# A graph network kernel on one Trainium2 core: paired filter loads and a reordered GRU stage

## The reference

```python
h = relu(_bn(_conv1d(xc, conv1_w, 0), ...))
h = _bn(_conv1d(h, conv2_w, 8), ...)              # 17 taps along the nodes
x_conv = transpose(relu(h + xc), (0, 2, 1))
s = x @ w_se.T + b_se                             # 3 columns
dist = sq[:, :, None] + sq[:, None, :] - 2.0 * einsum('bnd,bmd->bnm', s, s)
A = exp(-dist) * mask
msg = relu(x @ w_msg.T + b_msg)
x_nmp = einsum('bnm,bmd->bnd', A, msg)
x_in = concatenate([x_conv, x_nmp], axis=-1)
gi = x_in @ w_ih.T + b_ih
gh = x @ w_hh.T + b_hh
r, z = sigmoid(gi_r + gh_r), sigmoid(gi_z + gh_z)
nn_ = tanh(gi_n + r * gh_n)
x = _layernorm(x + (1.0 - z) * nn_ + z * x)
```

## Time and profile before

| | |
|---|---|
| median of 3 runs | 2246.25 us |
| profiled execution | 2246.6 us, span 2244.8 us |
| busy PE, PEld | 2039.8 us (91%), 1745.0 us (78%) |
| busy DVE, ACT, POOL | 1470.5 us (66%), 1175.7 us (52%), 676.7 us (30%) |
| product stage, first to last matmul start | 773.9 to 1007.6 us |
| GRU stage, first scores to end | 1021.8 to 2244.8 us |
| mean granted clock of TensorE | 0.974 of 2.4 GHz |

### The profile page before, as it was taken

How to read it: one execution, slowest core, us unless ns; L and a number is a source line. 1 busy time by engine, 2 the same in 40 slices (tenths; PEclk the granted TensorE clock), 3 DMA queues, 4 the chain that set the end, 5 groups by cost and what they waited for, 6 DMA issues and landing times.

```text
span 2244.8 us, 38042 instructions
## 1 busy us (share of the span) xinstructions
PE 2039.8 (91%) x11782; PEld 1745.0 (78%) x11782; DVE 1470.5 (66%) x2709; ACT 1175.7 (52%) x2174; POOL 676.7 (30%) x563
## 2 busy tenths in 40 slices
PE   6888788885988789884999999999999999999997
PEld 5877687774888677774888888888888888888886
DVE  5999797996777666654555655565656565555564
ACT  6888687874555566553344444444444444434342
POOL 5887686873000000000222222222222222222222
PEclk9999999997999999996999999999999999999999
DMA  4655565564222387774112112121212121212110
GB/s 143 220 203 203 191 211 212 213 220 168 80 80 84 88 238 231 230 211 160 45 58 75 66 66 74 58 77 54 78 53 78 53 78 53 78 53 80 67 38 19
DMA packets 208069, 263.07 MB, mean 117 GB/s; under 512 B 12939, under 2 KB 159089, under 8 KB 203761
## 3 DMA queue, kind: packets, MB, share of 16 engines
q1 hardware_dynamic: 207984, 262.14, 35.2%
HBM read 174.01 MB, written 88.08 MB: 117 GB/s over the span
## 4 chain that ended last, share of the span: by engine, by line
PE 52%; issue 1%; ACT 1%; DMA 1%; DVE 0%; SPq 0%; POOL 0%; POOLq 0%; ACTq 0%; DVEq 0%
PE c_ps_g L1386 36%; PE c_ps_s L1413 5%; PE c_ps_m L1386 4%; PE c_ps_s L1386 2%; PE c_ps_s L1457 1%; PE c_ps_y L1436 1%; PE c_ps_y L1473 1%; PE c_ps_m L1473 1%; DMA c_yf<-y_spec 1%; PE c_ps_m L1474 0%; PE c_ps_y L1474 0%; ACT c_wi_h L1147 0%; SPq L1038 0%; SPq L1046 0%; DVE c_t L1255 0%
## 5 line engine op out<-in xcount | busy, mean ns | idle before, releaser
L1209 POOL TENSOR_TENSOR c_cl<-c_xc,c_ch 128x512 fp32r<-128x512 f32 x64 | 82.6, 1291 | 488.2 <-ACT c_ch L1101 470.8
L1285 DVE TENSOR_SCALAR c_work<-c_work 128x512 f32<-128x512 f32 x64 | 27.4, 427 | 219.3 <-ACT c_work L1096 219.3
L833 PE MATMUL m_ps<-m_wh,m_xl 128*128 128x256 f32 (+1 forms) x406 | 136.4, 336 | 35.1 <-issue 16.8
L1386 PE MATMUL c_ps_g<-c_xh,c_wh_l 128*128 128x512 f32 x384 | 155.6, 405 | 4.2 <-POOL c_cl L1209 4.2
L1386 PE MATMUL c_ps_g<-c_ch,c_wi_l 128*128 128x512 f32 x384 | 153.9, 401 | 0.0
L1386 PE MATMUL c_ps_g<-c_xl,c_wh_h 128*128 128x512 f32 x384 | 152.4, 397 | 0.0
L1386 PE MATMUL c_ps_g<-c_ch,c_wi_h 128*128 128x512 f32 x384 | 152.1, 396 | 0.0
L1386 PE MATMUL c_ps_g<-c_nh,c_wi_l 128*128 128x512 f32 x384 | 151.9, 396 | 0.0
L1386 PE MATMUL c_ps_g<-c_xh,c_wh_h 128*128 128x512 f32 x384 | 151.9, 396 | 0.0
L1386 PE MATMUL c_ps_g<-c_cl,c_wi_h 128*128 128x512 f32 x384 | 151.7, 395 | 0.0
L1386 PE MATMUL c_ps_g<-c_nl,c_wi_h 128*128 128x512 f32 x384 | 151.7, 395 | 0.0
(11 more groups left out here) (226 smaller groups left out, 7095.9 us busy)
## 6 DMA issues: line engine op xcount, KB each, us to landing
w_spec<-a_spec SPq DMA_DIRECT2D x32, 1088.0 KB, 11.0
m_w<-w_spec SPq DMA_DIRECT2D x68, 512.0 KB, 3.8
a_xt<-in_x_t SPq DMA_DIRECT2D x64, 256.0 KB
a_xn<-in_x_n SPq DMA_DIRECT2D x64, 256.0 KB, 9.3
x_t<-a_x1t SPq DMA_DIRECT2D x64, 256.0 KB, 9.7
s_x<-x_t SPq DMA_DIRECT2D x64, 256.0 KB, 3.0
y_spec<-m_y SPq DMA_DIRECT2D x64, 256.0 KB, 2.4
c_x<-x_t SPq DMA_DIRECT2D x32, 512.0 KB, 3.9
```

The costliest lines, as they stand in the source:

```text
L833: last = nc.tensor.matmul(out.rearrange("p r (q c) -> p r q c", q=CHUNKS), xx[:, v, c, part], ww[:, v, c].rearrange("p q r c -> p r q c")[ ...
L1209: nc.gpsimd.tensor_tensor(cl[:, v, j], xc[:, j], ch[:, v, j].bitcast(F32), ALU.subtract).then_inc(s_cl, 1)
L1285: nc.vector.tensor_scalar(zz[:, :], tz[:, :], 0.5, 0.5, ALU.mult, ALU.add).then_inc(s_zz, 1)
L1386: last = nc.tensor.matmul(out, stationary, moving, start=(n == 0), stop=(n == len(passes) - 1))
```

## The change

In the product stage the filters of two slots are loaded at once (1 MB, 1 KB pieces in place of 512 B) into one of two buffers of a pair. The high and low parts get three buffers, so that the parts of slot s wait for the products of slot s - 3. In a step, ACT makes `m_xh` and `m_wh` before it copies `m_y`, and DVE makes `m_wl` before it subtracts. SP stores slot i - 5 in step i instead of slot i - 3. The unroll is 12 in place of 4.

In the GRU stage the inverse of one half is made of 256-column products: yh against the high and low parts of the transform side by side, yl against the high part, and the first four frequencies of two graphs in one product with 96 rows. It writes `c_ps_m` in place of `c_ps_s`. DVE adds its two halves in two operations onto x1 with the shift already added (`c_xs`, on ACT, behind the n tanh). DVE makes `c_cl`, and the result from three operations without POOL. The distances get 27 rows of fp32r in place of 9 of fp32, for which ACT makes high parts and DVE stacked rows. A gate takes the message part ahead of the x_conv part, with a wait of its own ahead of each in the first R gate. The first inverse stands behind the Z gate of half 0, the second behind IN of half 1.

```diff
-        w = sb("w", [P, BUFS, KD, CHUNKS, 2, CW])
-        wh = sb("wh", [P, 2, KD, CHUNKS, 2, CW], F32R)
...
+        w = sb("w", [P, BUFS // 2, KD, CHUNKS, 2, 2, CW])
+        wh = sb("wh", [P, SPLIT, KD, CHUNKS, 2, CW], F32R)
...
-                    sp.dma_start(w[:, u].rearrange("p t q r c -> p (t q) (r c)"),
-                                 w_spec.rearrange("n p d c -> p n d c")[:, :, bass.ds(2 * i, 2)].rearrange("p n d c -> p n (d c)")
-                                 ).then_inc(s_w[u], 16)
...
-                    s, b = i - 3, (u - 3) % BUFS
+                if u % 2 == 0 and live(0):
+                    reached(sp, s_wl, i - BUFS + 2)
+                    sp.dma_start(w[:, u % BUFS // 2].rearrange("p t q s r c -> p (t q) (s r c)"),
+                                 w_spec.rearrange("n p d c -> p n d c")[:, :, bass.ds(2 * i, 4)].rearrange("p n d c -> p n (d c)")
...
             def step(i, u, k, live):
+                if live(1):
+                    s, b, v = i - 1, (u - 1) % BUFS, (u - 1) % SPLIT
+                    reached(act, s_m, s - SPLIT + 1)
+                    nc.scalar.activation(xh[:, v], x_spec[:, :, bass.ds(s, 1)].rearrange("p c o r g -> p c (o r) g"), ACT.Copy).then_inc(s_xh, 1)
+                    reached(act, s_w[b // 2], (turns(k, u, 1) + 1) * 16)
+                    nc.scalar.activation(wh[:, v], w[:, b // 2, :, :, b % 2], ACT.Copy).then_inc(s_wh, 1)
...
                     nc.scalar.activation(y[:, b], ps[:, b, 0], ACT.Copy).then_inc(s_yc, 1)
-                if live(1):
-                    s, b, v = i - 1, (u - 1) % BUFS, (u - 1) % 2
-                    reached(act, s_m, s - 1)
-                    nc.scalar.activation(xh[:, v], x_spec[:, :, bass.ds(s, 1)].rearrange("p c o r g -> p c (o r) g"), ACT.Copy).then_inc(s_xh, 1)
-                    at_block = k if b <= u else k - 1
-                    reached(act, s_w[b], (at_block + 1) * 16)
-                    nc.scalar.activation(wh[:, v], w[:, b], ACT.Copy).then_inc(s_wh, 1)
...
+                    reached(dve, s_wh, s + 1)
+                    nc.vector.tensor_tensor(wl[:, v], w[:, b // 2, :, :, b % 2], wh[:, v].bitcast(F32), ALU.subtract).then_inc(s_wl, 1)
...
-                if live(1):
-                    s, b, v = i - 1, (u - 1) % BUFS, (u - 1) % 2
-                    reached(dve, s_wh, s + 1)
-                    nc.vector.tensor_tensor(wl[:, v], w[:, b], wh[:, v].bitcast(F32), ALU.subtract).then_inc(s_wl, 1)
...
+        RR = 3 * B * 2 * REST
...
+        ps_inv = ps_m.rearrange("p h (b s n) -> p (h b) s n", b=2, s=2)
...
+                for dst, src in ((di_raw[:, :], dft_i), (dr_raw[:, :], dft_r), (bn[:, :, :], bn2), (mk[:, :], masks)):
...
+                    for side, (row, high) in enumerate(((left, left_h), (right, right_h))):
+                        reached(act, s_lr, 2 * ga + side + 1)
+                        nc.scalar.activation(high[:, :], row[:, :], ACT.Copy).then_inc(s_lrh, 1)
...
+                    loaded(act, s_xg, 1, ga, v)
+                    reached(act, s_t2, 2 * KD * ga)
+                    for j in range(KD):
+                        nc.scalar.activation(xs[:, j], xg[:, v, j], ACT.Identity, bias=shift2[:, j:j + 1]).then_inc(s_xs, 1)
...
-                if live(3):
-                    g, w = i - 3, 1 - u
-                    loaded(pool, s_xg, 1, g, w)
-                    with_x(g, w, 0)
-                if live(2):
-                    ga, v = i - 2, u
-                    for j in range(KD):
-                        reached(pool, s_xc, KD * ga + j + 1)
-                        reached(pool, s_ch, KD * ga + j + 1)
-                        reached(pool, s_gz, 2 * ga - 2)
-                        nc.gpsimd.tensor_tensor(cl[:, v, j], xc[:, j], ch[:, v, j].bitcast(F32), ALU.subtract).then_inc(s_cl, 1)
-                if live(3):
-                    with_x(g, w, 1)
...
-                nc.vector.scalar_tensor_tensor(t2[:, j], ps_s[:, :], scale2[:, j:j + 1], xg[:, u, j], ALU.mult, ALU.add).then_inc(s_t2, 1)
-                reached(dve, s_t2, KD * g + j + 1)
                 reached(dve, s_cl, KD * (g - 1) + j + 1)
-                nc.vector.tensor_scalar(xc[:, j], t2[:, j], shift2[:, j:j + 1], 0.0, ALU.add, ALU.max).then_inc(s_xc, 1)
+                nc.vector.scalar_tensor_tensor(t2[:, j].rearrange("p (b n) -> p b n", b=B), halves[:, 0], scale2[:, j:j + 1],
+                                               xs[:, j].rearrange("p (b n) -> p b n", b=B), ALU.mult, ALU.add).then_inc(s_t2, 1)
+                reached(dve, s_t2, 2 * n + 1)
+                nc.vector.scalar_tensor_tensor(t2[:, j].rearrange("p (b n) -> p b n", b=B), halves[:, 1], scale2[:, j:j + 1],
+                                               t2[:, j].rearrange("p (b n) -> p b n", b=B), ALU.mult, ALU.add).then_inc(s_t2, 1)
...
+            def xconv_low(g, v, j):
+                reached(dve, s_ch, KD * g + j + 1)
+                reached(dve, s_gz, 2 * g - 2)
+                nc.vector.scalar_tensor_tensor(cl[:, v, j], t2[:, j], 0.0, ch[:, v, j].bitcast(F32), ALU.max, ALU.subtract).then_inc(s_cl, 1)
...
-                reached(dve, s_zd, n)
-                nc.vector.tensor_scalar(zz[:, :], tz[:, :], 0.5, 0.5, ALU.mult, ALU.add).then_inc(s_zz, 1)
-                reached(dve, s_dd, n + 1)
-                reached(dve, s_zz, n + 1)
                 reached(dve, s_yt, n)
-                nc.vector.tensor_tensor(zd[:, :], zz[:, :], dd[:, :], ALU.mult).then_inc(s_zd, 1)
-                reached(dve, s_nx, n + 1)
-                reached(dve, s_zd, n + 1)
+                loaded(dve, s_xg, 1, g, w)
+                nc.vector.scalar_tensor_tensor(xa, tz, 3.0, xg[:, w, j], ALU.add, ALU.mult).then_inc(s_xa, 1)
+                reached(dve, s_nn, n + 1)
+                nc.vector.scalar_tensor_tensor(nb, tz, 1.0, nn, ALU.subtract, ALU.mult).then_inc(s_nb, 1)
+                reached(dve, s_nb, n + 1)
                 reached(dve, s_y, g)
-                nc.vector.tensor_tensor(yt[:, j], zd[:, :], nx[:, :], ALU.add).then_inc(s_yt, 1)
+                nc.vector.tensor_tensor(yt[:, j], xa, nb, ALU.subtract).then_inc(s_yt, 1)
...
+                    for side, (row, high, stacked) in enumerate(((left, left_h, left_s), (right, right_h, right_s))):
+                        reached(dve, s_lrh, 2 * ga + side + 1)
+                        reached(dve, s_d, ga)
+                        nc.vector.scalar_tensor_tensor(stacked[:, :], high[:, :].bitcast(F32), mlow[:, side:side + 1], row[:, :],
...
+                    terms.append(((lambda k: wi_h[:, KD + k, cols]), (lambda k: wi_l[:, KD + k, cols]), nh, nl, (s_nl, 1)))
+                    terms.append(((lambda k: wi_h[:, k, cols]), (lambda k: wi_l[:, k, cols]), ch, cl, (s_cl, KD)))
+                count, total = 0, 3 * KD * len(terms)
+                for w_high, w_low, high, low, made in terms:
+                    if made is not None and sums_of is not None:
+                        reached(pe, made[0], made[1] * (sums_of + 1))
+                    for k in range(KD):
+                        for stationary, moving in ((w_low(k), high[:, v, k]), (w_high(k), low[:, v, k]), (w_high(k), high[:, v, k])):
+                            last = nc.tensor.matmul(out, stationary, moving, start=(count == 0), stop=(count == total - 1))
+                            count += 1
+                return last
...
+            def inverse(v, j):
...
-                    for n, (stationary, moving) in enumerate(passes):
-                        last = nc.tensor.matmul(ps_s[:, b * P:b * P + P], stationary, moving, start=(n == 0), stop=(n == len(passes) - 1))
+                for h in range(2):
+                    for b in range(2 * h, 2 * h + 2):
+                        nc.tensor.matmul(ps_inv[:, b], yh[:, b, cols], di[:, :, :], start=(b % 2 == 0), stop=False)
+                        nc.tensor.matmul(ps_inv[:, b, 0], yl[:, b, cols], di[:, 0], start=False, stop=False)
+                    last = nc.tensor.matmul(ps_inv[:, 2 * h:2 * h + 2, 0], yr[:, v, cols],
+                                            dr[:, h * D:h * D + D].rearrange("p (b n) -> p b n", b=2), start=False, stop=True)
                 last.then_inc(s_inv, 1)
...
                 if live(2):
-                    reached(pe, s_lr, 2 * ga + 2)
+                    reached(pe, s_yl, ga + 1)
+                    loaded(pe, s_yr, 3, ga, v)
+                    reached(pe, s_mpre, 2 * ga + 2)
+                    inverse(v, 0)
+                    reached(pe, s_lrs, 2 * ga + 2)
                     for b in range(B):
                         cols = slice(b * P, b * P + P)
-                        last = nc.tensor.matmul(ps_s[:, cols], left[:, cols], right[:, cols], start=True, stop=True)
+                        last = nc.tensor.matmul(ps_s[:, cols], left_s[:, cols], right_s[:, cols], start=True, stop=True)
...
+                    reached(pe, s_t2, 2 * (KD * ga + 1))
...
+                if live(2):
+                    reached(pe, s_ns, KD * ga + 1)
```

(33 more changed lines are left out.)

212 lines of the change are left out of this document (104 added, 108 removed).

## The result

The changed kernel takes 2165.6 us in the median of 4 runs (2163.5 to 2172.0), beside 2246.4 for the kernel before (2244.4 to 2247.2): a ratio of 0.9649, 95% interval 0.9636 to 0.9661. It is faster by 81 us where 95 were forecast. The time lies inside the stated range (2138 to 2172), but above the forecast's own (2140 to 2160). The profiled execution takes 2163.5 us, 83.1 less than the one of before.

What follows compares the result with a forecast made beforehand. PE bounds the GRU stage; in the product stage a chain over ACT and DVE holds PE up. 2246.6 - 34 (product stage) - 62 (GRU groups) + 1 + 0.3 (ends) = 2151.9, stated as 2151 us; 8-in-10 range 2138 to 2172.

Steps and rivals of the forecast that it cites:

- the first two rivals: Product stage: 1 MB loads bound it, 2171 us, chance 0.11; GRU stage: DVE chains late, about 2171 us, chance 0.10.
- the signs that the prediction names itself: Wrong if `m_wh` waits for load every second slot, PE waits in GRU loop, or 256-column inverse products exceed 0.17 us.
- Inverses, -1.20 us a group: GRU stage: both inverses fall from 3.52 to 2.32 us a group, each taking 1.16 us.
- Distances, -0.80 us a group: GRU stage: four fp32 products taking 1.29 us become 0.54 us in fp32r, restart included; -0.80 taken.
- -62: GRU stage: 2.00 us a group from inverses and distances, in 31 of 32 groups; period 35.0 us.
- DVE, ACT and the waits beside PE: GRU stage: DVE's 25.5 and ACT's 18.0 us of a 35.0 us period stay hidden, no PE wait met late.
- the rival on DVE's chains: GRU stage: late DVE chains make PE wait 0.5 to 0.8 us a group, +16 to +25 us; chance 0.10.
- Product stage, -34 us: Product stage: falls from 233.7 to 199 us, with slots of 2.83 us instead of 3.44.
- The terms 191, 1.5 and 6: Product stage: 191 us for slots without waits, 1.5 for the later first load, 6 for the start.
- The 8.1 us: Product stage: time available for a 1 MB filter load, which was to take 5.3 to 6.9 us.
- The first rival: Product stage: 1 MB loads bound it, slots of 3.12 to 3.2 us, +20 us, 2171 us; chance 0.11.
- Head and tail, +1.3: GRU stage's ends: +1 us (-1 to +4) before the first gates, +0.3 for the result at the end.

Runs made afterwards that it cites:

- two_splits: Changed kernel with single 512 KB filter loads, given two split buffers (high and low parts) instead of three: 2167.7 us, ratio 0.9651.
- narrow_inverse: Changed kernel with each 256-column product of the inverses made as two of 128 columns: 2192.4 us, ratio 0.9766.

## Why the prediction was right, and where it was off

The time lies in the stated range because that range was drawn wide enough for either of the first two rivals; the forecast's own range was missed by 6 us. By the signs that the prediction names itself, its product stage is wrong (`m_wh` waits for 29 of 34 loads, so in nearly every second slot), and its GRU stage is right but for the distances.

- **What bounds each stage**: right. PE had no wait in the GRU loop, and the sum of distances between matmul starts was the time. The product stage's chain over ACT and DVE was rightly read: it goes when a third split buffer gives it a slot (two_splits).
- **Inverses, -1.20 us a group**: right, 1.21 measured (1.16 us and, from the second one's rows, 1.15), and narrow_inverse shows that the wide shape does two thirds of it.
- **Distances, -0.80 us a group**: mis-sized, -0.50 measured. "four 128-column products at 0.111 are 0.44 us; with a restart of 0.10 it is 0.54" took the price from products of 128 rows. Those of 27 rows pause at either edge and are 0.147 apart; at 96 rows the four take 0.44. This is 0.3 x 31 = 9 us. With 2.00 replaced by 1.77 (1.71 from these two, 0.06 not placed), -62 becomes -55.
- **DVE, ACT and the waits beside PE**: right. DVE's durations, the sums per period and the absence of waits came as forecast, and the rival on DVE's chains fell.
- **Product stage, -34 us**: the slot of 2.83 was right (2.82), the load was mis-sized. (The terms 191, 1.5 and 6 make 198.5 and so -35; it was written down as -34.) "1 MB then takes 3.3 + 2.0 = 5.3 us, and up to 6.9" came out as 7.5 in the uneven course, with 10 us of gaps and a first product 2.4 us late instead of 1.5. The 8.1 us put against it were counted to where PE waits, not to where `m_wh` is due (6.0). What was put on the start, 6 us, was too much: with single loads the stage takes 773.3 to 967.0, 193.7 us, not the 197 that the working gives without the late first load. This error of 3 us hid as much of the gaps, by luck. So this term is -27, and -33 in the even course. The first rival was there in mechanism and at half its price.
- **Head and tail, +1.3**: the head is 0. From the first gate product to the end the kernel gained 56.2 us, of which the 31 periods are 54.9; a cost of 0.3 at the tail can't be told from that.

Together: 7.0 us are missing in the product stage and 5.5 from the first gate on (56.2 for 61.7), and the head's +1 didn't come. Unrounded this is 11.6 us, from the 2151.9 of the sum to the profiled 2163.5. The median run is 2 us slower than that, in the scatter of the paired loads. That packets of 1 KB are cheaper for each byte was right (0.781 x 16 x 220 us over 53920 packets of 1011 B is 51.0 ns in the changed kernel, 51.4 forecast for 1 KB), and the share is 0.84 in a stretch where single loads have 0.96. It bought nothing, since the DMA engines were not what PE waited for.
